# A causal mask moved from mask matmuls on TensorE to a GpSimd select after the exp, with new interleaving tables

## The chip, the cores and the metric

The kernel runs on one core of a Trainium2 chip. The metric is the device time of one execution in microseconds; "before" is the median of three runs.

## The reference, cut to what matters

The input is 16 sequences of 256 tokens with 128 channels, and it goes through nine residual layers: causal attention (16 heads of 8), a mixture of experts, causal attention, a grouped attention with a gated mixture of experts, linear attention, causal attention with an MLP, an arccos-kernel attention, and three blocks of quantised linear layers. Only the three causal attentions (stages `causal0`, `causal1`, `causal2`) are touched. Each computes, per head,

```python
a = einsum('bhqd,bhkd->bhqk', q, k) * hd ** (-0.5)
a = softmax(where(key > query, -1e9, a), axis=-1)
out = einsum('bhqk,bhkd->bhqd', a, v)
```

so what must be seen is that a probability is zero wherever its key is later than its query.

## The kernel before

**Passes and halves.** The sequences go in eight passes of two (512 tokens). Each pass has a FRONT list of stages (causal0, moe0, causal1, mqa, moe1) and a BACK list (linear, causal2, mlp, arccos, three blocks). The program has three parts: "fronts" (the fronts of two passes side by side), a loop of six turns called "both" (the front of one pass beside the back of another), and "backs" (two backs side by side). The two that run side by side are called halves; each has its own four PSUM banks and its own buffers.

**The order of work.** Each engine runs its instructions in program order. Every stage is a Python generator per engine that yields between steps, and `weave` takes steps from the two halves in turn by a table written out by hand for each engine and part (`PE_RUNS`, `ACT_RUNS`, `DVE_RUNS`): the numbers are how many steps come from one half, then from the other. A step contains its own semaphore waits, so a wait in one half's step holds up the other half's steps behind it on that engine.

**A causal stage.** It projects q, k and v, finds a row maximum for every query and head (`max_pe`, `max_dve`), and then works through 12 sets (`CSETS`) of three, three and two heads (`TRIOS`). A head has three score blocks of 128 keys by 128 queries: the earlier keys against both query tiles (256 columns), and the later keys against the later queries (128 columns), 384 columns in all (`HEADW`). Two of the three are diagonal blocks, in which half of the entries must be masked. For a set, `causal_scores_pe` waits until the exp of the set before has emptied the banks, writes the mask into the two diagonal blocks of each head by one bf16 matmul over 256 columns (line 837), and adds to it the scores (line 843) and the negated maximum (line 848). `causal_exp_act` (line 933) then takes the exp of all heads of the set in one ScalarE instruction, from PSUM into one of two `probs` buffers, and `causal_pv_pe` (lines 862 and 865) multiplies the probabilities by the values. On TensorE the step "probabilities by values" of set e-1 comes after the scores of set e, and the exp of set e+1 waits for it, since there are two buffers.

**GpSimd.** It only fills some constants at the start of the program.

## Time and profile before

| What | us |
|---|---|
| median of three runs | 3342.96 |
| lowest and highest | 3331.83, 3349.52 |
| profiled execution, span from first to last instruction | 3337.4 |
| TensorE matmul busy | 2641.8 |
| ScalarE busy | 1912.7 |
| VectorE busy | 1763.9 |
| GpSimd busy | 3.6 |
| mean granted TensorE clock, share of full speed | 0.795 |

The profiled execution's own time is given by its span alone, 5.6 us under the median of the runs. Matmuls are pipelined and their ends are modelled, so durations of neighbours overlap; the distance between two starts is the better measure of what one of them costs.

### The profile page before, as it was taken

What the parts mean: (1) busy time and instruction counts of PE and PEld (TensorE: products, weight loads), DVE (VectorE), ACT (ScalarE), POOL (GpSimd) and SP (SyncE); (2) the same over time, 40 slices, a digit from 0 to 9 for tenths busy, and PEclk for the clock granted to TensorE, in tenths of its full rate; (3) what the DMA queues carried; (4) which work ended last, traced back from release to release, by engine and by line L of the source; (5) the groups of instructions that cost most, each with busy time, mean ns of one, the idle gap of its engine ahead of it and who ended that gap; (6) DMA issues with size and microseconds to landing.
All of it is one profiled execution on the core that took longest, in us unless ns stands there. A gap on an engine that the chain in (4) does not pass through costs nothing.

```text
span 3337.4 us, 46425 instructions
## 1 busy us (share of the span) xinstructions
PE 2641.8 (79%) x18736; PEld 1529.0 (46%) x18736; DVE 1763.9 (53%) x2698; ACT 1912.7 (57%) x1960; POOL 3.6 (0%) x12
## 2 busy tenths in 40 slices
PE   8999999777997789877898688986889868897215
PEld 4666456343563435534355344553445534453102
DVE  5463574545656355553555545654455544563524
ACT  2433435875358753586445864468534685447994
POOL 0000000000000000000000000000000000000000
PEclk7997989659896588966899668986779867987557
DMA  3000000000000000000000000000000000000000
GB/s 128 2 1 1 20 1 1 1 1 8 1 1 1 1 8 1 1 1 0 8 1 1 1 0 8 2 1 1 0 5 2 1 1 0 4 1 1 0 0 6
DMA packets 4561, 18.68 MB, mean 6 GB/s; under 512 B 608, under 2 KB 864, under 8 KB 3808
## 3 DMA queue, kind: packets, MB, share of 16 engines
q1 hardware_dynamic: 4320, 15.38, 1.2%
q8 instruction: 162, 2.65, 0.3%
q14 instruction: 79, 0.65, 0.1%
HBM read 13.28 MB, written 2.10 MB: 5 GB/s over the span
## 4 chain that ended last, share of the span: by engine, by line
PE 54%; ACT 19%; DVE 15%; issue 12%; DVEq 0%; DMA 0%; ACTq 0%; SPq 0%
ACT back_cosines L1320 6%; PE one_ps L1164 2%; PE two_ps L1275 2%; PE one_ps L862 2%; PE two_ps L910 2%; ACT back_cosines L1322 2%; PE one_ps L1710 2%; DVE back_nsum L1330 2%; PE one_ps L1717 2%; ACT L1320 2%; PE one_ps L766 1%; PE one_ps L1723 1%; DVE back_cosines L1393 1%; ACT L1862 1%; PE two_ps L862 1%
## 5 line engine op out<-in xcount | busy, mean ns | idle before, releaser
L1320 ACT ACTIVATE back_cosines<-back_cosines 128x2048 f32<-128x2048 f32 x256 | 472.2, 1899 | 0.5
L933 ACT ACTIVATE front_scratch<-one_ps 128x1152 f32<-128x1152 f32 x168 | 171.5, 1021 | 225.0 <-PE one_ps L848 224.8
L1322 ACT ACTIVATE back_cosines<-back_cosines,wts 128x2048 f32<-128x2048 f32 x128 | 252.4, 1994 | 41.1 <-DVE back_cosines L1393 40.9
L1330 DVE TENSOR_REDUCE back_nsum<-back_cosines 128x8 f32<-128x2048 f32 x64 | 144.4, 2281 | 234.0 <-ACT back_cosines L1320 234.0
L797 DVE TENSOR_REDUCE front_negm<-one_ps 128x8 f32<-128x1024 f32 (+1 forms) x168 | 204.4, 1220 | 56.6 <-PE one_ps L772 55.5
L837 PE MATMUL one_ps<-ident_bf,mask_q 128*128 128x256 bf16 x480 | 93.3, 302 | 80.5 <-ACT front_scratch L933 69.3
L696 ACT ACTIVATE back_cosines<-two_ps,wts 128x512 fp32r<-128x512 f32 x28 | 19.3, 688 | 224.1 <-PE two_ps L910 224.1
L766 PE MATMUL one_ps<-front_qkr 32*128 32x128 f32 (+1 forms) x896 | 136.5, 414 | 14.1 <-issue 8.9
L1393 DVE TENSOR_SCALAR back_cosines<-two_ps 128x2048 f32<-128x2048 f32 x56 | 128.2, 2290 | 28.5 <-PE two_ps L1257 28.3
L933 ACT ACTIVATE back_cosines<-two_ps 128x1152 f32<-128x1152 f32 (+1 forms) x84 | 86.0, 1024 | 92.0 <-PE two_ps L848 92.0
L766 PEld LDWEIGHTS one_ps<-front_qkr 32*128 32x128 f32 x896 | 96.6, 274 | 88.5 <-DVE front_negm L797 46.3
L1275 PE MATMUL two_ps<-back_cosines,back_vs 128*18 128x256 f32 x896 | 79.5, 505 | 69.0 <-DVE back_vs L1342 69.0
L862 PE MATMUL one_ps<-front_scratch,one_v 128*18 128x256 f32 x896 | 116.7, 424 | 6.1 <-DVE front_split_parts L704 5.7
L772 PE MATMUL one_ps<-mask_q,ident_bf 128*128 128x512 bf16 (+1 forms) x360 | 119.4, 428 | 0.0
L843 PE MATMUL one_ps<-front_qkr 32*128 32x256 f32 (+1 forms) x896 | 105.8, 328 | 0.0
L797 DVE TENSOR_REDUCE back_cosines<-two_ps 128x4 f32<-128x1024 f32 (+1 forms) x84 | 97.9, 1216 | 8.8 <-PE two_ps L772 8.6
L837 PEld LDWEIGHTS one_ps<-ident_bf,mask_q 128*128 128x128 bf16 x480 | 39.2, 103 | 132.7 <-ACT front_scratch L933 92.1
L700 DVE TENSOR_SCALAR front_scratch<-one_ps,wts 128x512 fp32r<-128x512 f32 x77 | 57.4, 746 | 71.6 <-PE one_ps L865 56.0
L910 PE MATMUL two_ps<-back_cosines,two_v 128*18 128x128 f32 x896 | 77.8, 376 | 20.9 <-DVE back_split_parts L704 20.6
L1164 PEld LDWEIGHTS one_ps<-front_v,front_scratch 128*128 128x128 f32 x448 | 85.0, 291 | 13.0 <-issue 13.0
L953 DVE TENSOR_TENSOR back_cosines<-two_ps,wts 128x768 f32<-128x768 f32 (+1 forms) x84 | 72.6, 864 | 34.8 <-PE two_ps L883 34.8
L843 PEld LDWEIGHTS one_ps<-front_qkr 32*128 32x128 f32 x896 | 71.3, 208 | 42.1 <-issue 42.1
(630 smaller groups left out, 5795.1 us busy)
## 6 DMA issues: line engine op xcount, KB each, us to landing
wts<-w_dram SPq DMA_DIRECT2D x1, 4184.0 KB, 15.3
front_xin<-x_dram SPq DMA_DIRECT2D x8, 256.0 KB, 4.2
out_dram<-back_z SPq DMA_DIRECT2D x8, 256.0 KB, 2.1
wts<-w_dram SPq DMA_DIRECT2D x1, 1736.5 KB, 19.1
wts<-w_dram SPq DMA_DIRECT2D x1, 1199.0 KB, 5.3
wts<-w_dram SPq DMA_DIRECT2D x1, 1152.0 KB, 16.5
wts<-w_dram SPq DMA_DIRECT2D x3, 256.0 KB, 5.8
wts<-w_dram SPq DMA_DIRECT2D x1, 516.5 KB, 4.8
```

The lines of the kernel that those rows point to most:

```text
L766: nc.tensor.matmul(h.ps[:, j, gi * keys:(gi + 1) * keys], h.q4r[rows(j, QUAD), g0 + gi, b * SEQ + qt * P:b * SEQ + (qt + 1) * P], h.k4r[ro ...
L797: nc.vector.tensor_reduce(into, h.ps[:, js, :].rearrange("p j (g k) -> p j g k", k=keys), AX.X, ALU.max, negate=True).then_inc(h.max_done. ...
L843: nc.tensor.matmul(h.ps[:, k, into], h.k4r[rows(j, QUAD), g, keys], h.q4r[rows(j, QUAD), g, queries], start=False, stop=False, skip_group_ ...
L862: nc.tensor.matmul(h.ps[rows(j, V2), 3, b * SEQ:(b + 1) * SEQ], h.v18[:, 2 * b, GROUPS * j + g, :], h.probs[:, e % 2, k * HEADW:k * HEADW ...
L910: last = nc.tensor.matmul(h.ps[rows(j, V2), 3, b * SEQ + t * P:b * SEQ + (t + 1) * P], h.v18[:, 2 * b + t, GROUPS * j + g, :], h.probs[:, ...
L933: nc.scalar.activation(h.probs[:, e % 2, 0:n * HEADW].rearrange("p (k c) -> p k c", c=HEADW), h.ps[:, 0:n, 0:HEADW], ACT.Exp, scale=float( ...
L1164: last = nc.tensor.matmul(h.ps[:, 3, c:c + MV1], h.probs[:, (e - 1) % 2, w:w + P], h.v33[:, 2 * b + kt, :], start=(kt == 0), stop=(kt == 1 ...
L1275: last = nc.tensor.matmul(h.ps[rows(j, V2), 2 + g2, 0:SEQ], h.vs[:, kt, HPG * g2 + j, :], h.cosines[:, u % 2, w:w + SEQ], start=(kt == 0), ...
L1320: nc.scalar.activation(cosines, cosines, func, scale=scale).then_inc(h.arc_pass.sem, 1)
L1322: nc.scalar.activation(cosines, cosines, func, scale=scale, bias=C(bias)).then_inc(h.arc_pass.sem, 1)
L1330: nc.vector.tensor_reduce(h.nsum[:, kt, :].rearrange("p (g2 j) -> p j g2", g2=2), h.cosines[:, u % 2, kt * 4 * TOK:(kt + 1) * 4 * TOK].rea ...
L1393: nc.vector.tensor_scalar(h.cosines[:, u % 2, kt * 4 * TOK:(kt + 1) * 4 * TOK].rearrange("p (j t) -> p j t", j=HPG), h.ps[:], CLIP, CLIP_L ...
```

## The change

The mask matmuls of line 837 go. The score matmuls now start the accumulation themselves, and the first of them writes its 256 columns into blocks 0 and 2 of the bank, so that blocks 0 and 1 are the two diagonal ones. The exp writes the probabilities of a set with all diagonal blocks side by side at the front of the buffer (`p (t k q)`), unmasked. A new GpSimd step, `causal_keep_pool`, waits for the exp, sets the entries with a key later than the query to zero with one `affine_select` in place over the diagonal blocks (768 elements per partition for three heads, 512 for two), and raises a new semaphore `probs_kept`. The step that multiplies by the values waits for that semaphore in place of the exp's; the next set's scores still wait for the exp's. All tables of TensorE, ScalarE and VectorE are replaced, with the same number of steps in each, and GpSimd gets one. The part of the diff that isn't shown is the rest of these tables and the two unused generators for stages without work on GpSimd.

```diff
     "both": (
-        1, 2, 1, 1, 1, 1, 1, 1, 1, 1, 2, 1, 1, 2, 2, 2, 1, 2, 1, 1, 1, 3, 1, 2, 2, 1, 1, 3, 1, 2, 1, 5, 2, 1, 1,
-        2, 1, 2, 1, 1, 2, 1, 2, 1, 1, 2, 2, 2, 1, 2, 1, 1, 1, 2, 1, 2, 1, 1, 1, 2, 3, 2, 2, 1, 3, 2, 1, 2, 1, 2,
-        2, 2, 1, 2, 1, 2, 1, 4, 1, 3, 1, 4, 1, 1, 1, 1, 1, 3, 1, 1, 2, 1, 4, 3, 2, 4, 3, 1, 1, 1, 2, 4, 2, 1, 1,
-        1, 1, 4, 1, 4, 26, 1, 2, 2, 3, 2, 7, 1, 3, 2, 1, 2, 22, 2, 5, 1, 1, 1, 1, 5, 2, 2, 1, 1, 2, 1, 4, 1, 4,
-        2, 3, 1, 2, 1, 10, 1, 2, 2, 3, 1, 3, 1, 5, 1,
+        1, 2, 1, 1, 1, 1, 1, 1, 1, 1, 2, 1, 1, 3, 1, 2, 1, 5, 2, 1, 1, 2, 1, 2, 1, 2, 1, 2, 1, 2, 1, 2, 1, 1, 2,
+        2, 1, 2, 1, 1, 3, 1, 2, 1, 1, 1, 1, 1, 2, 3, 1, 3, 1, 1, 1, 1, 2, 2, 1, 1, 1, 1, 2, 2, 3, 1, 2, 6, 1, 2,
+        2, 2, 1, 1, 1, 4, 1, 4, 1, 4, 1, 1, 1, 4, 1, 1, 3, 1, 4, 2, 1, 1, 1, 3, 3, 2, 2, 1, 2, 4, 2, 2, 1, 1, 1,
+        5, 1, 2, 30, 1, 1, 2, 2, 2, 9, 1, 1, 2, 2, 1, 1, 1, 18, 2, 5, 1, 1, 1, 1, 3, 2, 1, 1, 4, 2, 1, 7, 1, 1,
+        2, 4, 1, 1, 1, 11, 1, 3, 2, 1, 2, 8, 1,
...
+POOL_RUNS = {
+    "fronts": (
+        7, 1, 1, 1, 1, 1, 1, 1, 2, 8, 5, 3, 2, 2, 3, 1, 1, 1, 1, 4, 2, 5, 2,
+    ),
+    "both": (
+        12, 12, 16,
+    ),
+    "backs": (
+        8, 2, 1, 1, 1, 4, 2, 5,
     ),
 }
...
+        self.probs_kept = signal("probs_kept", {s: CSETS for s in CAUSAL})
...
+        def score_tile(h, k, kt):
+
+
+            return h.ps[:, k, 0:HEADW].rearrange("p (n q) -> p n q", q=P)[:, 0:3:2, :] if kt == 0 else h.ps[:, k, P:2 * P]
+
+        def prob_tile(h, e, k, kt):
+
+
+            n = TRIOS[e % len(TRIOS)]
+            tiles = h.probs[:, e % 2, 0:n * HEADW].rearrange("p (t k q) -> p t k q", k=n, q=P)
+            return tiles[:, 0:3:2, k, :] if kt == 0 else tiles[:, 1, k, :]
+
         def causal_scores_pe(pe, h, turn, s):
             for e in range(CSETS + 1):
                 yield
...
-                    for k in range(len(heads)):
-                        diagonals = h.ps[:, k, :].rearrange("p (n q) -> p n q", q=P)[:, 0:4:2, :]
-                        nc.tensor.matmul(diagonals, mask_q[:], ident_bf[:].unsqueeze(1).broadcast_to([P, 2, P]),
-                                         start=True, stop=False, skip_group_check=True)
-                    for kt, into in ((0, slice(0, SEQ)), (1, slice(SEQ, HEADW))):
+                    for kt in range(2):
                         for k, (b, j) in enumerate(heads):
                             queries = slice(b * SEQ + kt * P, (b + 1) * SEQ)
                             keys = slice(b * SEQ + kt * P, b * SEQ + (kt + 1) * P)
-                            nc.tensor.matmul(h.ps[:, k, into], h.k4r[rows(j, QUAD), g, keys], h.q4r[rows(j, QUAD), g, queries],
-                                             start=False, stop=False, skip_group_check=True)
+                            nc.tensor.matmul(score_tile(h, k, kt), h.k4r[rows(j, QUAD), g, keys], h.q4r[rows(j, QUAD), g, queries],
+                                             start=True, stop=False, skip_group_check=True)
                         for k, (b, j) in enumerate(heads):
                             queries = slice(b * SEQ + kt * P, (b + 1) * SEQ)
                             minus_max = max_rows[rows(j, QUAD), g:g + 1].broadcast_to([QUAD, P])
-                            last = nc.tensor.matmul(h.ps[:, k, into], minus_max, h.maxTr[rows(j, QUAD), queries],
+                            last = nc.tensor.matmul(score_tile(h, k, kt), minus_max, h.maxTr[rows(j, QUAD), queries],
...
         def causal_pv_pe(pe, h, turn, s, e):
             g, heads = trio(e)
             yield
-            pe.wait_ge(h.probs_ready.sem, h.probs_ready.at(turn, s, e + 1))
+            pe.wait_ge(h.probs_kept.sem, h.probs_kept.at(turn, s, e + 1))
             if e % len(TRIOS) == 0:
                 if g > 0:
                     pe.wait_ge(h.part_ready.sem, h.part_ready.at(turn, s, g))
             for k, (b, j) in enumerate(heads):
                 nc.tensor.matmul(h.ps[rows(j, V2), 3, b * SEQ:(b + 1) * SEQ], h.v18[:, 2 * b, GROUPS * j + g, :],
-                                 h.probs[:, e % 2, k * HEADW:k * HEADW + SEQ], start=(b == 0), stop=False, skip_group_check=True)
+                                 prob_tile(h, e, k, 0), start=(b == 0), stop=False, skip_group_check=True)
             for k, (b, j) in enumerate(heads):
                 last = nc.tensor.matmul(h.ps[rows(j, V2), 3, b * SEQ + P:(b + 1) * SEQ], h.v18[:, 2 * b + 1, GROUPS * j + g, :],
-                                        h.probs[:, e % 2, k * HEADW + SEQ:(k + 1) * HEADW],
+                                        prob_tile(h, e, k, 1),
                                         start=False, stop=True, skip_group_check=True)
             last.then_inc(h.pv_ps.sem, 1)
 
@@ -930,8 +950,28 @@
                 act.wait_ge(h.score_ps.sem, h.score_ps.at(turn, s, e + 1))
                 if e >= 2:
                     act.wait_ge(h.pv_ps.sem, h.pv_ps.at(turn, s, e - 1))
-                nc.scalar.activation(h.probs[:, e % 2, 0:n * HEADW].rearrange("p (k c) -> p k c", c=HEADW),
-                                     h.ps[:, 0:n, 0:HEADW], ACT.Exp, scale=float(HD) ** -0.5).then_inc(h.probs_ready.sem, 1)
+                nc.scalar.activation(h.probs[:, e % 2, 0:n * HEADW].rearrange("p (t k q) -> p k t q", k=n, q=P),
+                                     h.ps[:, 0:n, 0:HEADW].rearrange("p k (t q) -> p k t q", q=P), ACT.Exp,
+                                     scale=float(HD) ** -0.5).then_inc(h.probs_ready.sem, 1)
+
+        def causal_keep_pool(pool, h, turn, s):
+
+
+            for e in range(CSETS):
+                n = TRIOS[e % len(TRIOS)]
+                yield
+                pool.wait_ge(h.probs_ready.sem, h.probs_ready.at(turn, s, e + 1))
+                pool.sem_inc(wait_carrier)
+                diagonals = h.probs[:, e % 2, 0:2 * n * P].rearrange("p (n q) -> p n q", q=P)
+                nc.gpsimd.affine_select(diagonals, diagonals, pattern=[[0, 2 * n], [1, P]], compare_op=ALU.is_ge, fill=0.0,
+                                        base=0, channel_multiplier=-1).then_inc(h.probs_kept.sem, 1)
+
+        def headed_pool(pool, h, turn, s):
+            if s in CAUSAL:
+                yield from causal_keep_pool(pool, h, turn, s)
+
+        def nothing_pool(pool, h, turn, s):
+            yield from ()
...
+            run(pool, POOL_RUNS, {"norm": nothing_pool, "causal": headed_pool, "linear": headed_pool, "mqa": nothing_pool,
+                                  "moe0": nothing_pool, "moe1": nothing_pool, "mlp": nothing_pool, "arccos": nothing_pool,
+                                  "block": nothing_pool})
```

## Rows read from the trace of the kernel before

**Rows 1.** The page: busy time of each engine, and the chain's shares

```profile
PE 2641.8 (79%) x18736; PEld 1529.0 (46%) x18736; DVE 1763.9 (53%) x2698; ACT 1912.7 (57%) x1960; POOL 3.6 (0%) x12
...
PE 54%; ACT 19%; DVE 15%; issue 12%; DVEq 0%; DMA 0%; ACTq 0%; SPq 0%
```

**Rows 2.** Windows, all instructions: start:end length, busy and count of each engine, clock

```profile
core 0: us, PE busy (x) PEld busy (x) DVE busy (x) ACT busy (x) POOL busy (x), PEclk, DMA share, GB/s
0.00:480.00 480.00, 436.98 (x3308) 272.34 (x3311) 263.04 (x466) 174.80 (x240) 3.56 (x12) 0.88 0.07 27
892.00:1304.00 412.00, 337.35 (x2362) 194.27 (x2358) 220.86 (x337) 241.05 (x247) 0.00 (x0) 0.79 0.01 2
2950.00:3337.00 387.00, 190.54 (x1300) 93.18 (x1300) 170.30 (x208) 292.27 (x235) 0.00 (x0) 0.69 0.01 2
```

**Rows 3.** Windows, line 837 (the mask matmuls) alone

```profile
0.00:480.00 480.00, 26.10 (x144) 12.24 (x144) 0.88 0.07 27
892.00:1304.00 412.00, 18.13 (x96) 7.57 (x96) 0.79 0.01 2
2950.00:3337.00 387.00, 11.66 (x64) 5.83 (x64) 0.69 0.01 2
sum 3337.00, PE 143.82 PEld 62.15; mean PE 17.98 PEld 7.77
```

**Rows 4.** Line 837: what TensorE sat idle for ahead of it

```profile
  ACT front_scratch L933: 165.8, 113
```

**Rows 5.** Timeline of two sets at the upper clock: start, length, instruction

```profile
501.05 0.50 PE L837 MATMUL two_ps<-ident_bf,mask_q 128*128 128x256 bf16 x3
501.48 0.39 PE L843 MATMUL two_ps<-back_qkr 32*128 32x256 f32 x3
...
502.09 0.62 PE L862 MATMUL two_ps<-back_cosines,two_v 128*18 128x256 f32 x6
502.20 1.13 ACT L933 ACTIVATE back_cosines<-two_ps 128x1152 f32<-128x1152 f32 x1 [0.90 <-PE two_ps L848]
...
503.51 0.39 PE L837 MATMUL two_ps<-ident_bf,mask_q 128*128 128x256 bf16 x2
```

**Rows 6.** The chain that ended last, 500 to 520: start, length, instruction

```profile
503.58 0.33 PE two_ps L837 x2
...
504.51 0.55 PE two_ps L862 x6
505.06 0.22 PE two_ps L865 x6
```

**Rows 7.** Timeline of a set at the lower clock

```profile
1041.53 0.82 PE L837 MATMUL one_ps<-ident_bf,mask_q 128*128 128x256 bf16 x3 [6.73 <-ACT front_scratch L933]
...
1042.28 0.58 PE L843 MATMUL one_ps<-front_qkr 32*128 32x256 f32 x3
...
1043.33 1.05 PE L862 MATMUL one_ps<-front_scratch,one_v 128*18 128x256 f32 x6
```

**Rows 8.** Windows of one turn of the loop, line 837 alone

```profile
1032.00:1052.00 20.00, 3.07 (x11) 0.98 (x11) 0.50 0.00 0
1052.00:1072.00 20.00, 3.61 (x19) 1.36 (x19) 0.88 0.01 2
1072.00:1092.00 20.00, 0.39 (x2) 0.11 (x2) 0.72 0.01 1
```

**Rows 9.** Windows of the same turn, all instructions, columns as in group 2

```profile
912.00:932.00 20.00, 18.98 (x197) 11.66 (x193) 9.00 (x30) 10.68 (x14) 0.00 (x0) 1.00 0.01 2
1032.00:1052.00 20.00, 10.82 (x85) 6.04 (x87) 4.47 (x4) 19.97 (x13) 0.00 (x0) 0.50 0.00 0
1052.00:1072.00 20.00, 16.49 (x213) 9.38 (x209) 15.65 (x16) 13.07 (x11) 0.00 (x0) 0.88 0.01 2
```

**Rows 10.** Timeline of GpSimd, all of whose work is at the start

```profile
0.74 1.06 POOL L1926 MEMSET one_v<- 128x1152 f32 x1 [0.29 <-POOLq L2093]
1.73 0.53 POOL L1927 MEMSET front_negm<- 128x512 f32 x1
```

**Rows 11.** Line 953, VectorE: duration ns min/median/max, first and last start, forms

```profile
L953 DVE TENSOR_TENSOR back_cosines<-two_ps,wts x84: 678/946/958, 420.2 to 2903.8; 128x768 f32<-128x768 f32 x56, 128x512 f32<-128x512 f32 x28
```

2 lines of the change are left out of this document (added), and 68 rows, old and new, of tables (ACT_RUNS, DVE_RUNS, PE_RUNS).

## The prediction

> **What bounds the kernel now.** I read the page first: TensorE is busy for four fifths of the span, ScalarE and VectorE for little more than half, GpSimd for nothing, and the chain that ended last lies on TensorE for 54%, on ScalarE for 19%, on VectorE for 15% [rows 1]. That is a mean over parts with different limits, so next came the windows. In "fronts" (0 to 480) TensorE is busy 437 of 480 us and bounds. A turn of the loop takes 412 us (892 to 1304 is the one I read), with TensorE at 337 and ScalarE at 241. "Backs" has TensorE at 191 of 387 and ScalarE at 292 [rows 2]. Inside the turn, at 912 to 932, TensorE is busy 18.98 of 20 us, while at 1032 to 1052, where causal1 runs beside the long exp passes of the arccos stage, it is ScalarE with 19.97 of 20 and TensorE has 10.82 [rows 9]. The reader is to see two kinds of place for a causal set: one where TensorE has no idle time, and one where its next set waits for a ScalarE that is busy with the other half.
>
> Then the line that goes: line 837 is busy 143.8 us in all, 26.1 in fronts, 18.1 in each full turn, 11.7 in backs [rows 3]. TensorE idled 165.8 us ahead of it for the exp of the front half's set before [rows 4]. So the mask matmuls stand in a loop of their own: exp, masks, scores, exp.
>
> **Removed: 768 mask matmuls.** The busy time overstates them, since matmuls overlap. From the first mask matmul to the first score matmul three of them take 501.48 - 501.05 = 0.43 us at full clock; their busy time is 0.50 [rows 5]. The chain gives two of them 0.33 us [rows 6]. At the lower clock three take 1042.28 - 1041.53 = 0.75 [rows 7]. Taking 0.07 off each of the 288 sets (3 stages x 8 passes x 12), 143.8 - 20.2 = 123.6 us of TensorE's time goes: 26.1 - 54 x 0.07 = 22.3 in fronts (144 mask matmuls are 54 sets), 11.66 - 24 x 0.07 = 10.0 in backs, and 91.3 in the loop. It is a maximum only if nothing else waits. Where does it count?
> - Fronts: TensorE bound for 91% of the time; 20 us.
> - Loop: of the 18.1 us in a turn, 3.07 lie at 1032 to 1052, where ScalarE is full: nothing comes of them. 4.00 more lie at 1052 to 1092 [rows 8], with ScalarE at 13.07 of 20 in the first half of it [rows 9]: I count half. That leaves (18.1 - 3.1 - 2.0) / 18.1 = 0.72 of 91.3, so 66 us.
> - Backs: the causal sets end there before the long ScalarE passes; 8 of 10 us.
> Together 94 us.
>
> **Added: 288 selects, and a wait.** The select has its engine to itself, so what counts is how late it makes the step on lines 862 and 865, and what stands behind that step in TensorE's queue: everything of both halves, the next scores included. The trace of before has no select. Below: GpSimd's memsets take 1.06 us for 1152 elements and 0.53 for 512 [rows 10], 0.83 ns an element, so 768 take 0.74. A select reads as well, so it is no faster. Above: three such passes (read, compare, write), 0.10 + 3 x 0.64 = 2.0; VectorE's 768-element pass with a second input takes 0.95 [rows 11], and twice that is 1.9. I take 1.1 us, between the same engine's row and twice it, nearer the first because the memset is a row of this engine; 0.74 and 2.0 stay for the range. To this I add 0.35 us for two semaphores, from the exp to GpSimd and from there to TensorE: an estimate, twice the 0.18 us from the end of an exp (502.20 + 1.13) to the matmul that waited for it (503.51) [rows 5].
>
> What does it do to a set? With full clock and three heads: scores until the next step 502.09 - 501.48 = 0.61, from the last of them to the exp 0.11, exp 1.13 [rows 5], values step 0.77 [rows 6]. Let w be the other half's work per set on TensorE. Before, a set takes the larger of 0.18 + 0.43 + 0.61 + 0.11 + 1.13 = 2.46 (the loop through the exp) and 1.81 + w (TensorE full). After, if nothing stands between the scores of e and the values step of e-1, that step can start 0.11 + 1.13 + 0.35 + S after the end of the scores of e-1, where S is the select, and the set takes the largest of 2.03, 1.38 + w, and half of (1.59 + S + 1.38 + w). For S = 1.1 and w = 0, 0.5 and 1 that is 2.04, 2.29 and 2.54 against 2.03, 2.03 and 2.38 without the wait: 0.14 us lost on average. For S = 0.74 it is 0.03, for S = 2.0 it is 0.59.
>
> How many sets have nothing between? That can be counted in the new table of TensorE, by writing out both halves' steps in its order: in the loop 21 of 33 such places in a turn (4 in causal0, 9 in causal1, 8 in causal2), 22 of 44 in fronts, 5 of 22 in backs, so 22 + 6 x 21 + 5 = 153. (By the old table 25, 37 and 18.) The others have at least one step of the other half between and I cost them at nothing; that step is the cover, and where it is taken away the set joins the 153 at 0.14 us. 153 x 0.14 = 22 us.
>
> The Trainium skill, "GPSIMD Engine Reference", section "Performance pitfalls for Q7 kernels", gives 1.03 to 2.03 cycles an element for a compare and select; at its 1.2 GHz an estimate of 0.66 to 1.30 us for 768 elements, by which the loss would be about 2 to 37 us. No run shown here has one.
>
> **Moved, at nothing.** The exp reads and writes the same elements in runs of 128, so its 1.13 us stays. Values steps read two runs of 128 columns where they read one of 256: same columns. VectorE and ScalarE keep their steps in number. The new tables as such are worth something I can't take from rows; I count zero and keep 25 us either way for them, about a fourth of what is at stake.
>
> Sum against the profiled execution: 3337.4 - 94 + 22 = 3265; the median is 5.6 us higher, which makes 3271. I say 3270.
>
> **Rivals.**
> 1. The select is slow, two passes or more. For it: the engine has done nothing but memsets here, and 1.9 us is twice VectorE's row. At S = 2.0 the loss is 153 x 0.59 = 90 us and the gain is gone: 3339. The Trainium skill, "GPSIMD Engine Reference", section "When to use GPSIMD", has VectorE about twice as fast for elementwise work with two inputs, and GpSimd near its line rate for one; by the first rule the select would be this rival, by the second it would not.
> 2. The other side, slower: from S = 2.0 on each further 0.1 us costs 153 x 0.05 = 8 us, and the covered sets begin to stall too. At S = 2.6 it is 153 x 0.89 = 136 us lost: 3343 - 94 + 136 = 3385. TensorE would show a wait for GpSimd ahead of most values steps.
> 3. The freed time isn't free: ScalarE's passes and VectorE's steps set the end in more of the loop than I counted, or the new tables don't use the gaps. For it: 165.8 us of idle time ahead of line 837, which is latency and not TensorE work. Against: that idle time is in the same loop that gets shorter by the masks. A third of the 94 us remains: 3312 without a stall, about 3323 with half of it.
> 4. The clock. The masks are dense work, and a TensorE that waits for GpSimd is idle in short pieces. At 912 to 932 it has 1.00 at 95% busy, at 1032 to 1052 it has 0.50 (1.2 GHz) at 54% [rows 9]. A set's scores take 1043.33 - 1042.28 = 1.05 us at the lower level [rows 7] against 0.61, and its values step about double 0.77: 1.2 us more for each set that changes level. 60 sets that do so cost the 72 us of the forecast: 3343.
>
> **How the numbers follow.** Forecast, S from 0.74 to 1.5 (where the formula gives 0.34 us a set, 52 us in all, and 3301): 0.72. Rival 1: 0.08. Rival 2: 0.06. Rival 3: 0.09. Rival 4: 0.05. A change of 0.5% is 17 us, about what a measurement of this kernel can tell from none. The forecast is all faster; of rival 3 0.04 is faster and 0.05 the same; rival 1 is the same; rival 2 and 0.04 of rival 4 are slower. That makes 0.76, 0.14 and 0.10. The range goes down to all 124 us and the tables' 25, 3343 - 149 = 3194, and I cut it at 3200; up it takes in rivals 1 and 3, to 3345. The likeliest case alone has 3225 to 3315.
>
> **What would show it.** The profile after should have no bf16 matmul in the score step, GpSimd busy 288 x about 1.0 = 290 us (between 200 and 520), a set of scores 0.43 us shorter, the turn of the loop at about 404 us in place of 412, fronts at about 463, and waits of line 862 for GpSimd of 30 us or so in total. If the select's mean is under 0.8 us the time should be below 3260; over 2 us, the prediction is wrong by step "added". If the select is short and the time isn't down, rival 3 holds, and if the mean clock falls below 0.77 in the loop, rival 4.

## The result, and the profile after

The changed kernel takes 3421.53 us (median; 3419.33 to 3425.81) against 3339.53 of the kernel before in the same session: a ratio of 1.0237, 95% interval [1.0207, 1.0266]. It is 2.4% slower. The prediction was 3270 us with a range up to 3345.

The page after, busy times and the chain that ended last, in the form of [rows 1]:

```profile
span 3419.3 us, 45758 instructions
PE 2627.1 (77%) x17968; PEld 1512.0 (44%) x17968; DVE 1768.7 (52%) x2698; ACT 1931.7 (56%) x1980; POOL 232.9 (7%) x300
...
PE 53%; DVE 19%; ACT 18%; issue 9%; POOL 0%; DVEq 0%; DMA 0%; ACTq 0%; POOLq 0%; SPq 0%
```

TensorE has its 768 instructions fewer, but only 14.7 us less busy time than in [rows 1], where the mask matmuls were busy for 143.8 [rows 3]. GpSimd has 0% of the chain (0.9 us in a turn of the loop); VectorE's share went from 15% to 19%. ScalarE has 20 instructions more, though no step was added on it.

The selects, grouped by shape (mean ns of one; idle time and releaser behind the bar), the longest of them in the timeline with the VectorE pass beside it, and what TensorE sat idle for ahead of the values step (the source view of its first line: us, times):

```profile
L966 POOL TENSOR_SCALAR_AFFINE_SELECT front_scratch<-front_scratch 128x768 f32<-128x768 f32 x128 | 110.8, 866 | 2297.9 <-ACT front_scratch L953 2297.8
L966 POOL TENSOR_SCALAR_AFFINE_SELECT front_scratch<-front_scratch 128x512 f32<-128x512 f32 x64 | 40.7, 637 | 141.2 <-ACT front_scratch L953 141.2
L966 POOL TENSOR_SCALAR_AFFINE_SELECT back_cosines<-back_cosines 128x512 f32<-128x512 f32 x32 | 22.6, 707 | 60.9 <-ACT back_cosines L953 60.9
...
971.82 2.29 DVE L1595 TENSOR_TENSOR front_qk<-front_split_parts,front_oh 128x2048 f32<-128x2048 f32 x1
972.21 2.40 POOL L966 TENSOR_SCALAR_AFFINE_SELECT back_cosines<-back_cosines 128x512 f32<-128x512 f32 x1 [3.55 <-ACT back_cosines L953]
...
  POOL front_scratch L966: 31.9, 42
...
  POOL back_cosines L966: 12.9, 34
```

So a select is 0.87 us for three heads and 0.64 for two (the mean of 0.71 in one group comes from a single one of 2.40 us beside a VectorE pass over two tensors), below the 1.1 that the prediction took. It holds TensorE up in 76 places for 44.8 us, of which next to nothing is in the chain. That speaks against the select as what made the kernel slower, and the experiments below settle it. Where the time went is read from SyncE's queue, which loads an input when the opening stretch ends and stores an output once a turn (start us, length):

```profile
430.01 0.34 SPq L1933 DMA_DIRECT2D front_xin<-x_dram  x1
840.33 0.36 SPq L1938 DMA_DIRECT2D out_dram<-back_z  x1
...
1260.17 0.35 SPq L1938 DMA_DIRECT2D out_dram<-back_z  x1
...
2509.45 907.81 SPq L1938 DMA_DIRECT2D out_dram<-back_z  x4
```

In the kernel before the same four stand at 403.12, 807.63, 1216.90 and 2442.80. The opening stretch ("fronts") is 27 us longer, and the four turns between the first store and the fifth take (2509.45 - 840.33) / 4 = 417.3 us each against 408.8. What follows the fifth store, 909.9 us against 894.6, still holds the last turn.

### The profile page after: what moved, and what is told of

Its sections match the earlier page's. It is cut to its first block, busy times and chain, and to the rows that moved or that the text cites. A ratio compares the mean times of both kernels' runs of the same rounds, so it can differ in the third digit from the quotient of the medians.

```text
span 3419.3 us, 45758 instructions
## 1 busy us (share of the span) xinstructions
PE 2627.1 (77%) x17968; PEld 1512.0 (44%) x17968; DVE 1768.7 (52%) x2698; ACT 1931.7 (56%) x1980; POOL 232.9 (7%) x300
## 4 chain that ended last, share of the span: by engine, by line
PE 53%; DVE 19%; ACT 18%; issue 9%; POOL 0%; DVEq 0%; DMA 0%; ACTq 0%; POOLq 0%; SPq 0%
ACT back_cosines L1360 5%; ACT back_cosines L1362 3%; PE one_ps L778 3%; PE one_ps L882 3%; PE two_ps L1315 2%; PE one_ps L784 2%; PE one_ps L1204 2%; DVE back_cosines L1433 2%; DVE back_nsum L1370 2%; DVE front_negm L809 2%; PE two_ps L569 2%; PE two_ps L930 2%; PE one_ps L863 2%; PE one_ps L1750 2%; ACT L1360 1%
## 5 line engine op out<-in xcount | busy, mean ns | idle before, releaser
L966 POOL TENSOR_SCALAR_AFFINE_SELECT front_scratch<-front_scratch 128x768 f32<-128x768 f32 (+1 forms) x192 | 151.4, 790 | 2439.1 <-ACT front_scratch L953 2439.0
L863 PE MATMUL one_ps<-front_qkr 32*128 32x256 f32 (+1 forms) x896 | 118.0, 355 | 49.5 <-ACT front_scratch L953 35.5
L1315 PE MATMUL two_ps<-back_cosines,back_vs 128*18 128x256 f32 x896 | 96.6, 604 | 76.5 <-DVE back_vs L1382 76.5
L882 PE MATMUL one_ps<-front_scratch,one_v 128*18 128x256 f32 x896 | 137.0, 491 | 17.0 <-POOL front_scratch L966 8.5
L778 PEld LDWEIGHTS one_ps<-front_qkr 32*128 32x128 f32 x896 | 99.2, 280 | 88.6 <-DVE front_negm L809 45.2
L863 PEld LDWEIGHTS one_ps<-front_qkr 32*128 32x128 f32 x896 | 80.6, 232 | 109.8 <-ACT front_scratch L953 62.9
L966 POOL TENSOR_SCALAR_AFFINE_SELECT back_cosines<-back_cosines 128x768 f32<-128x768 f32 (+1 forms) x96 | 78.0, 813 | 416.2 <-ACT back_cosines L953 416.2
L1204 PEld LDWEIGHTS one_ps<-front_v,front_scratch 128*128 128x128 f32 x448 | 94.4, 321 | 18.4 <-issue 18.4
L1204 PE MATMUL one_ps<-front_v,front_scratch 128*128 128x33 f32 x448 | 97.8, 394 | 4.3 <-DVE front_scratch L1126 4.3
L868 PE MATMUL one_ps<-front_maxTr,max_rows 32*128 32x256 f32 (+1 forms) x896 | 96.8, 329 | 0.0
```

The source lines that it names most:

```text
L778: nc.tensor.matmul(h.ps[:, j, gi * keys:(gi + 1) * keys], h.q4r[rows(j, QUAD), g0 + gi, b * SEQ + qt * P:b * SEQ + (qt + 1) * P], h.k4r[ro ...
L863: nc.tensor.matmul(score_tile(h, k, kt), h.k4r[rows(j, QUAD), g, keys], h.q4r[rows(j, QUAD), g, queries], start=True, stop=False, skip_gro ...
L882: nc.tensor.matmul(h.ps[rows(j, V2), 3, b * SEQ:(b + 1) * SEQ], h.v18[:, 2 * b, GROUPS * j + g, :], prob_tile(h, e, k, 0), start=(b == 0), ...
L966: nc.gpsimd.affine_select(diagonals, diagonals, pattern=[[0, 2 * n], [1, P]], compare_op=ALU.is_ge, fill=0.0, base=0, channel_multiplier=- ...
L1204: last = nc.tensor.matmul(h.ps[:, 3, c:c + MV1], h.probs[:, (e - 1) % 2, w:w + P], h.v33[:, 2 * b + kt, :], start=(kt == 0), stop=(kt == 1 ...
```

## The experiments

All times below are ratios to the kernel before on the same chip and in the same session, since its median moved between 3337.6 and 3345.2; 0.001 is 3.3 us. "Front end" is the input load that ends "fronts", "turn" the mean of four turns, both from the one profiled execution of each run. That execution can lie off the median: for e1 it was the fastest of ten, 19 us under it. And the front end of e6, whose tables for fronts are the old ones, is 13 us later than that of e1. So small differences in these two columns carry little.

| run | median us | ratio, 95% interval | front end | turn |
|---|---|---|---|---|
| changed kernel | 3421.5 | 1.0237 [1.0207, 1.0266] | 430.0 | 417.3 |
| e1 select, old tables | 3344.3 | 1.0014 [0.9992, 1.0036] | 400.9 | 408.8 |
| e2 masks, new tables | 3465.6 | 1.0385 [1.0348, 1.0421] | 439.7 | 422.1 |
| e3 neither, old tables | 3302.4 | 0.9900 [0.9866, 0.9934] | 398.6 | 403.6 |
| e4 neither, new tables | 3423.7 | 1.0246 [1.0221, 1.0271] | 439.0 | 417.2 |
| e5 e1 with filler matmuls | 3345.6 | 1.0028 [1.0006, 1.0051] | 396.0 | 409.7 |
| e6 new tables in the loop alone | 3401.6 | 1.0182 [1.0147, 1.0218] | 413.5 | 418.1 |
| e7 new tables in fronts alone | 3367.5 | 1.0060 [1.0037, 1.0083] | 430.4 | 407.8 |
| e8 changed kernel, half the row maximum | 3411.0 | 1.0232 [1.0176, 1.0289] | 435.1 | 413.0 |
| e9 e1, half the row maximum | 3293.4 | 0.9896 [0.9841, 0.9951] | 388.9 | 401.9 |
| e10 loop new, then old | 3358.5 | 1.0046 [1.0025, 1.0067] | 400.1 | 413.0 |
| e11 loop old, then new | 3373.2 | 1.0084 [1.0055, 1.0113] | 395.3 | 413.9 |
| e12 e1, three places | 3633.5 | 1.0879 [1.0855, 1.0904] | 445.1 | 448.9 |
| e13 masks, three places | 3683.7 | 1.1029 [1.0996, 1.1063] | 447.2 | 453.1 |
| e14 e1, ScalarE's later order new | 3474.6 | 1.0415 [1.0385, 1.0445] | 400.9 | 431.5 |
| e15 neither, three places | 3630.6 | 1.0867 [1.0838, 1.0897] | 436.7 | 449.7 |
| e16 e1, values one step later | 3518.7 | 1.0533 [1.0500, 1.0565] | 419.8 | 433.5 |
| e17 three places, values behind scores | 3582.8 | 1.0734 [1.0703, 1.0764] | 446.0 | 441.2 |
| e18 changed kernel, one stretch put back | 3413.6 | 1.0239 [1.0201, 1.0277] | 437.4 | 413.9 |

**Mask, select and tables taken apart (e1 to e4).** e1 is the changed kernel with the TensorE, ScalarE and VectorE tables of before; e2 the kernel before with the new ones; e3 and e4 have neither mask nor select and wait for the exp directly:

```diff
-            pe.wait_ge(h.probs_kept.sem, h.probs_kept.at(turn, s, e + 1))
+            pe.wait_ge(h.probs_ready.sem, h.probs_ready.at(turn, s, e + 1))
```

> The code of the changed kernel with the order tables of before for TensorE, ScalarE and VectorE; GpSimd's table gives the selects in the order in which the old table of ScalarE has the exps. Theory T (the new tables lost the time, the select itself saves some): 3250 to 3310 us, faster than before by 1 to 3%. Theory W (the values step's wait for the select is the cause, whatever the order): 3400 us or more, since the old tables have 136 + 6 x 1 more places with nothing between the scores and the values step. Theory M (the masks were never on the path and the tables are neutral): 3340.

> The code of before, with its mask matmuls and no select, in the new order of TensorE, ScalarE and VectorE. Theory T: the masks come on top of a worse order, 3440 to 3520 us. Theory W: no wait for a select, so about 3340. Theory M: as the changed kernel or less, 3340 to 3420.

> Old tables, no mask matmuls and no select at all: the probabilities stay unmasked, and the values step waits for the exp. This is the most that taking the masks away can give in the old order. By my sum it should be 94 us under before, 3245. Theory T: 3230 to 3280. Theory W: the same, with the select variant far above it. Theory M: 3340.

> New tables, no mask matmuls and no select: the probabilities stay unmasked, and the values step waits for the exp. The difference from the changed kernel is the price of the wait for the select in the new order. Theory T: small, 3380 to 3410. Theory W: the whole loss and the masks' time come back, 3250 to 3300.

Measured: the new tables cost 0.0385 with masks, 0.0346 with neither and 0.0223 with the select: 129, 116 and 74 us. That is the loss, and it needs no select. In the old order, removing the masks brings 33 us (e3) and the select takes 38 of them back (e1 against e3). In the new order the masks' removal brings 46 us and the select costs nothing (e4 against the changed kernel, intervals overlap). Theory T holds for where the loss is, but not for its gain: e1 was to be 1 to 3% faster than before and is level with it, and e3 was to be at 3230 to 3280 and is at 3302. Theory M's 3340 is met by e1 alone; e2 and e3 rule it out.

The two orders can be compared with the same instructions in both. In the profiled executions of before and e2 TensorE is busy for 2641.8 and 2697.2 us and idle for 695.6 and 765.5: of 125 us more, 55 are longer matmuls and 70 are idle time. For e3 and e4 it is 81 and 48 of 129.

Why 33 us, where the masks were busy for 143.8? Line groups of TensorE, before, in e3 and after (busy us, mean ns of one), with the source view of the values line before and after (ns min/median/max):

```profile
L862 PE MATMUL one_ps<-front_scratch,one_v x896: 376/391/634, 59.9 to 2722.3; 128*18 128x256 f32 x180
...
L862 PE MATMUL one_ps<-front_scratch,one_v 128*18 128x256 f32 x896 | 116.7, 424 | 6.1 <-DVE front_split_parts L704 5.7
L843 PE MATMUL one_ps<-front_qkr 32*128 32x256 f32 (+1 forms) x896 | 105.8, 328 | 0.0
```

```profile
L882 PE MATMUL one_ps<-front_scratch,one_v 128*18 128x256 f32 x896 | 126.0, 455 | 15.6 <-DVE front_split_parts L716 15.6
L863 PE MATMUL one_ps<-front_qkr 32*128 32x256 f32 (+1 forms) x896 | 113.5, 339 | 87.1 <-ACT front_scratch L953 76.5 <-DVE front_maxTr L716 9.8
```

```profile
L882 PE MATMUL one_ps<-front_scratch,one_v x896: 376/392/634, 62.5 to 2778.4; 128*18 128x256 f32 x180
...
L882 PE MATMUL one_ps<-front_scratch,one_v 128*18 128x256 f32 x896 | 137.0, 491 | 17.0 <-POOL front_scratch L966 8.5 <-DVE front_split_parts L716 8.0
L863 PE MATMUL one_ps<-front_qkr 32*128 32x256 f32 (+1 forms) x896 | 118.0, 355 | 49.5 <-ACT front_scratch L953 35.5 <-DVE front_maxTr L716 13.3
```

The mean of the same matmuls got longer: a values matmul took 424 ns, 455 without masks, 491 after. Minimum, median and maximum stayed at 376, 391 and 634, so it isn't that each got longer: more of them run at the lower of the two clock levels (0.50, as in [rows 9]). Of the 1536 values matmuls over 256 columns, 154 take over 600 ns before, 308 in e3, 291 in e2, 428 in e4, 365 in e1 and 456 after, and nearly all others about 385. Before, all 154 began while the granted clock was 0.50 and none of the others did; after, it was so for 443 of the 456 and for 13 of the others (counted in the traces). TensorE's busy time fell by 2641.8 - 2557.9 = 83.9 us in e3 and not by 143.8. Some 20 of the missing 60 are the overlap that the prediction took off itself; the line groups of all other matmuls add up to 36 us more than before. And of the 83.9 not all is time won: TensorE's idle time rose from 695.6 to 740.7 us. Three windows over the same stretch of "fronts", of before, e3 and after (columns of [rows 2], last but two the granted clock), show what goes with it:

```profile
12.00:403.00 391.00, 366.19 (x2750) 232.69 (x2749) 211.35 (x389) 144.16 (x200) 0.00 (x0) 0.89 0.05 18
```

```profile
12.00:403.00 391.00, 363.91 (x2627) 231.58 (x2625) 210.97 (x389) 147.04 (x205) 0.00 (x0) 0.86 0.06 21
```

```profile
12.00:403.00 391.00, 353.56 (x2562) 228.35 (x2561) 196.81 (x368) 137.34 (x192) 37.70 (x48) 0.82 0.04 17
```

TensorE is as busy in e3 as before with 123 matmuls fewer, at 0.86 of full speed and not 0.89. "Fronts", for which the prediction counted 20 us, got 403.1 - 398.6 = 4.5 shorter.

**Does the clock hold the rest (e5)?** Three bf16 matmuls over 256 columns, adding zero to the values bank, ahead of TensorE's wait for the exp in 7 of 12 sets of e1, 504 in all:

```diff
                     else:
+                        if e % 3 != 1:
+                            for k in range(3):
+                                nc.tensor.matmul(h.ps[:, 3, 0:SEQ], zero_bf[:].broadcast_to([P, P]), ident_bf[:].unsqueeze(1).broadcast_to([P, 2, P]),
+                                                 start=False, stop=False, skip_group_check=True)
                         pe.wait_ge(h.probs_ready.sem, h.probs_ready.at(turn, s, e))
```

> The select with the old tables (3344 us), and ahead of the scores' wait for the exp, in 7 of 12 sets, three bf16 matmuls of 256 columns of zeros added into the values bank, which change nothing in it. They cost 0.43 us of TensorE at the upper clock, 168 sets, 72 us in all, but stand where TensorE often idles for the exp (211 us in all). Theory C (without the masks TensorE spends more of the causal stages at the lower clock, and that gives back most of what their removal saves): mean clock up from 0.782 to about 0.80 and the time within 15 us of 3344. Rival (the clock plays no part, the masks only filled idle time): clock as before, time up by 20 to 50 us.

The mean clock went from 0.782 to 0.798 (the medians over the runs of each are 0.777 and 0.793). A values matmul is back at the 424 ns of before, and 156 of 1536 take over 600 ns:

```profile
L886 PE MATMUL one_ps<-front_scratch,one_v 128*18 128x256 f32 x896 | 116.1, 424 | 22.8 <-DVE front_split_parts L716 16.1 <-POOL front_scratch L970 6.7
```

TensorE was busy for 2595.3 us against e1's 2591.3, although the filler alone is 89.4 of it: the other matmuls took 85 us less. Its idle time is 735 us against 732, so the filler didn't fill idle time; the clock that it bought paid for it, and no more. The time is e1's (1.0028 and 1.0014, intervals overlap). So dense work in these places raises the clock, and the masks did the same; but to raise it with filler brings nothing. Whether filler would help in the new order was not run.

**Which part of the tables (e6, e7).**

> The changed kernel with the new tables in the loop alone, the old ones in fronts and backs. By the turns in the traces (417.3 against 408.8 us) the new loop order costs 6 x 8.5 = 51 of the 77 us: 3395. If the loss is in fronts and backs: 3350 to 3365.

> The select code with the new tables in the opening stretch of two fronts alone, old ones in the loop and the backs. The x load that ends that stretch came at 430.0 us with all new tables and at 400.9 with the old ones, so this run should be slower by that: 3365 to 3375 us. If the order of the opening stretch costs nothing by itself and the 29 us come from what it hands to the loop, 3340 to 3350.

Against e1 the loop's tables cost 0.0168 (56 us), those of fronts 0.0046 (15 us; in the profiled executions the front end is 29 us later). Together that is 0.0214 of the 0.0223, so the backs' tables cost nothing that shows.

**Are VectorE's row maxima now in the way (e8, e9)?** In the new order the matmuls of the maxima (lines 778 and 784 on TensorE) lie on the chain for about 31 us a turn against 12, VectorE's reduces behind them for about 10 in both. Both runs leave out half of the columns of each reduce and leave the matmuls as they are:

```diff
-                nc.vector.tensor_reduce(into, h.ps[:, js, :].rearrange("p j (g k) -> p j g k", k=keys),
+                nc.vector.tensor_reduce(into, h.ps[:, js, :].rearrange("p j (g k) -> p j g k", k=keys)[:, :, :, 0:keys // 2],
```

> The changed kernel, but the row maximum is taken over half of the columns only, so a reduce of 1.22 us takes about 0.68 (the softmax's shift is another one and the output with it). VectorE loses about 150 us of work. Theory D (the new order puts the reduces of VectorE on the path): 60 to 100 us faster than the changed kernel, 3320 to 3360. Rival (the new order loses by TensorE's own idle and clock): about 20 to 40 us faster, as in the old order.

> The same half reduce in the select kernel with the old tables (3344 us). Theory D: 20 to 40 us faster, 3305 to 3325, half or less of what it brings in the new order. Rival: the same gain in both orders.

A theory that fell: it gains nothing that can be told in the new order (1.0232 against 1.0237) and 39 us in the old one (0.9896 against 1.0014). So it isn't VectorE's reduces that the new order suffers from. The matmuls, which are what grew on the chain, were not changed in any run.

**Which part of a turn (e10, e11).** One table for each engine that changes from one order to the other where the front half is in moe0 and the back half at the start of mlp.

> The select code with the old tables outside the loop and, in each turn of it, the new order of TensorE, ScalarE and VectorE up to the point where the front half is in moe0 and the back half at the start of mlp (that is, through causal0 and causal2), and the old order from there on (arccos, causal1, mqa, moe1 and the blocks); GpSimd's table is the new one of the loop. Theory L, that the new order is good where it goes around the select and loses its time in the stages behind: the new order was 1 to 4 us ahead of the old one at that point of a turn (129 against 132 us for the last exps of causal2), so a turn comes to 405 to 408 us against 408.8 with the old order all through, and the kernel to 3320 to 3345 us. Rival G, that the loss comes from the front and back halves' causal stages as laid out anew (its later part only shows what was displaced): the turn stays near 417 us and the time at 3390 to 3400. Rival E, that any order fitted to one part is only good with its other part: over 3360 us in this run and in the converse one.

> The converse: select code, old tables outside the loop, in each turn the old order through causal0 and causal2 and the new one behind it (arccos, causal1, mqa, moe1, blocks), GpSimd's old table. Theory L: all of the loop's loss is here, so about 3395 to 3410 us, turn near 417 to 420, and the count of function-table loads on ScalarE rises by most of the 20 that the new tables add. Rival G: near 3345 us with a turn of 409. Rival E: over 3400 here and over 3360 in the converse run.

The second part loses 0.0070 (23 us). The first loses 0.0032 (11 us), with intervals that just overlap; the new order isn't the better one there, and the second part alone is at 3373 us and not at the 3395 to 3410 of theory L. So L is wrong in its first half and has the second too large. The rest of the loop's loss, 0.0168 - 0.0102 = 0.0066 (22 us), appears only when both parts are new.

**Is it ScalarE's order there (e14, e18)?** The new order makes ScalarE change its function table more often, without any step being added: line groups of e1 and of the changed kernel,

```profile
L1360 ACT ACT_TABLE_LOAD x48 | 61.6, 1283 | 0.9
L1775 ACT ACT_TABLE_LOAD x27 | 34.6, 1283 | 1.3 <-PE one_ps L1750 0.9
```

```profile
L1360 ACT ACT_TABLE_LOAD x56 | 71.8, 1283 | 1.0
L1775 ACT ACT_TABLE_LOAD x33 | 42.3, 1283 | 7.6 <-PE one_ps L1750 7.2
```

188 loads in all against 168, 1.283 us each: 25.7 us. One place is where the front half's mqa begins. ScalarE's timeline there, in the changed kernel and then in e1 (line 1360 is an arccos pass of the back half, 1213 and 1217 mqa's copies of q and v):

```profile
1133.94 0.61 ACT L607 ACTIVATE front_sq<-front_sq 128x512 f32<-128x512 f32 x1
1134.58 1.28 ACT L1360 ACT_TABLE_LOAD   x1
1135.87 5.51 ACT L1360 ACTIVATE back_cosines<-back_cosines 128x2048 f32<-128x2048 f32 x3
1141.39 1.28 ACT L1360 ACT_TABLE_LOAD   x1
1142.69 1.91 ACT L1360 ACTIVATE back_cosines<-back_cosines 128x2048 f32<-128x2048 f32 x1
1144.51 0.58 ACT L1213 ACTIVATE front_qk<-one_ps 128x512 f32<-128x512 f32 x1
1144.98 0.27 ACT L1217 ACTIVATE front_v<-one_ps 128x128 f32<-128x128 f32 x1
```

```profile
1093.63 0.61 ACT L607 ACTIVATE front_sq<-front_sq 128x512 f32<-128x512 f32 x1
1094.27 1.28 ACT L1360 ACT_TABLE_LOAD   x1
1095.56 1.91 ACT L1360 ACTIVATE back_cosines<-back_cosines 128x2048 f32<-128x2048 f32 x1
1097.38 0.58 ACT L1213 ACTIVATE front_qk<-one_ps 128x512 f32<-128x512 f32 x1
1097.85 1.90 ACT L1360 ACTIVATE back_cosines<-back_cosines 128x2048 f32<-128x2048 f32 x1
1099.65 0.27 ACT L1217 ACTIVATE front_v<-one_ps 128x128 f32<-128x128 f32 x1
```

From the norm's last step to the copy of v it is 11.0 us in the new order and 6.0 in the old. VectorE's first maxima of mqa, in the same turn of each, come 306.2 and 298.7 us after the store that begins the turn (302.8 and 298.6 in the next one), behind 7.13 and 1.58 us of idle time:

```profile
1146.57 1.29 DVE L1240 TENSOR_REDUCE front_negm<-one_ps 128x2 f32<-128x512 f32 x2 [7.13 <-PE one_ps L1164]
```

```profile
1100.72 1.29 DVE L1240 TENSOR_REDUCE front_negm<-one_ps 128x2 f32<-128x512 f32 x2 [1.58 <-PE one_ps L1164]
```

> The select code with old tables, except that in each turn ScalarE's order alone is the new one behind causal0 and causal2; TensorE and VectorE keep the old order. With the new order of all three there the kernel took 3373 us, 29 more than with the old, and had 12 more loads of a function table on ScalarE (15.4 us). If the loads, or ScalarE's order as such, are the cause: 12 more loads here too, and 3360 to 3375 us. If TensorE's or VectorE's order is: 3340 to 3350, with or without the loads.

> The changed kernel with one stretch of ScalarE's order in the loop as it was before: where the front's mqa begins. In the changed kernel ScalarE runs four of the back's arccos passes (1.9 us each) and an extra load of its function table (1.28 us) between the norm ahead of mqa and mqa's copies of q and v, so that VectorE's maxima for mqa begin 303.1 us into a turn against 298.2 in the old order; until there the new order is not behind. The four passes go back to one ahead of the copy of q and one between q and v. Theory S (this place makes the loss of the loop's later part, 29 us over six turns in the run old then new): the turn comes from 417.3 down to about 412.5, function-table loads fall by 6 to 12, and the time by 25 to 35 us, to 3387 to 3400. Rival P (TensorE's and VectorE's new orders lose as much, and ScalarE's place is only where it shows): within 10 us of the changed kernel, 3410 to 3425.

e14 has 12 more loads and is 0.0401 (134 us) slower than e1: ScalarE's new order behind TensorE's and VectorE's old one is far worse than all three new (e11, 23 us). Its outcome is outside both expectations, and it tells no more than that the three tables are one thing. e18, with the stretch put back as it was, has 6 loads fewer and a turn of 413.9 instead of 417.3, 3.4 us; but its front end was 437.4 against 430.0 in a part that it doesn't touch, and the ratio, 1.0239, is the changed kernel's, as rival P has it. The place costs some 3 us a turn by the trace, a third of the 8.5, and the times don't show it. Theory S, with 25 us or more, fell.

**Can the select be hidden (e12, e13, e15 to e17)?** Sets of three, three and two heads fill 8 x 384 = 3072 columns, just the `probs` buffer, so that three places fit. In e12, e13 and e15 the values of set e-2 follow the scores of e, with the scores one step of the table earlier:

```diff
-            for e in range(CSETS + 1):
-                yield
+            for e in range(CSETS + 2):
+                if e <= CSETS:
+                    yield
...
-                if e > 0:
-                    yield from causal_pv_pe(pe, h, turn, s, e - 1)
+                if e > 1:
+                    yield from causal_pv_pe(pe, h, turn, s, e - 2)
```

> The select code with the old tables, and three places for the probabilities in turn instead of two (they fit in the same buffer, since sets of 3, 3 and 2 heads come in turn), with the values step of a set issued one set later: scores of e+2, then values of e. The select of a set then runs beside the next set's exp instead of ahead of a step that TensorE is at. Theory W (the select's 42 us in the old order, 3344 against 3302 with neither mask nor select, are its latency in the chain exp, select, values): most of it goes, 3300 to 3315 us, faster than the kernel before; waits of the values step for GpSimd fall to near nothing, select still about 0.87 us each. Rival C (the select's price is the clock, which is lower where TensorE has less to do, or GpSimd taking SBUF time from VectorE): still 3340 to 3350. Rival D (the later values step holds up the part that VectorE takes from its bank, and the group's end comes later): over 3350.

> The kernel before (mask matmuls, no select) with the same three places and the values step one set later: the control. Nothing stands between exp and values there, so theory W expects little, 3325 to 3345 us; if the later values step helps by itself (TensorE no longer waits for an exp ahead of values), it is up to 20 us faster, and then the gain of the run with the select is to be read less this.

> Neither mask nor select (the output is not causal within diagonal blocks), old tables, with the three places and the later values step: the floor for the run with the select. Theory W: equal to the two-place run without mask (3302 us) within 10, and the select run lies within 10 us above it.

With a set's time between exp and values the select costs 0.0012, 4 us with overlapping intervals (e12 against e15), where in e1 it cost 38. Theory W expected that, and says that the 38 us are latency ahead of the values step. That isn't shown. The select costs nothing in the changed kernel either, where nothing was put between. And e1 and e3, which differ by the select alone, have TensorE idle for 731.9 and 740.7 us and busy for 2591.3 and 2557.9 with the same 17968 matmuls: e1 waits for GpSimd ahead of the values in 56 places, 23.4 us in all, half of the changed kernel's 44.8, and what is longer is its matmuls, at a clock of 0.782 and not 0.787 (medians over the runs 0.777 and 0.786). So what the select costs in the old order reaches the time mostly as longer matmuls at a lower clock; why it does so there and not in the new order is open. One difference can be seen: in e1 six selects of the back half take 1.6 to 2.3 us, each beside a pass of VectorE over 2048 elements of two tensors (lines 1590 and 1595, 2.29 us), in the changed kernel one. That is some 7 us of GpSimd, too little for 38 by itself.

The shift itself costs 290 us (e12 against e1), and with the masks in place of the select 344 (e13 against before, for which theory W expected 3325 to 3345). Each scores step now stands where its exp may not be done, and 290 us is about one exp (1.02 us) for each of 288 sets; that this is the reason is argued and not shown.

e16 and e17 leave the scores where they were and move only the values, in e16 to the head of the next scores step (two places), in e17 behind its scores (three places):

```diff
+                if e > 1:
+                    causal_pv_pe(pe, h, turn, s, e - 2)
                 if e < CSETS:
...
-                    yield from causal_pv_pe(pe, h, turn, s, e - 1)
+                    yield
+                if e == CSETS:
+                    causal_pv_pe(pe, h, turn, s, e - 1)
```

> The select code with the old tables and two places for the probabilities. Every scores step stays where it is in TensorE's order; the values of a set are issued one step of the table later, at the head of the step that holds the next scores, so that what TensorE waits for there (the exp of the set after) is later than the select of this one. In the run with three places the scores had moved ahead by one step, to where their exp was not ready, and the loop's turn went from 409 to 449 us; with that shift the select cost nothing (3633 against 3631 without it). Theory W: with scores where they were, the select's 42 us go and little comes in its place: 3300 to 3325 us, faster than the kernel before. Rival D: the values now stand between TensorE and the scores in every set, 0.6 us of matmuls that ran beside an exp before, and VectorE gets each part of the output later: 3345 to 3400.

> As the run of values in the next step, but with three places for the probabilities and the values issued behind the scores of the same step, so that they run beside the exp that these scores release. Theory W: 3295 to 3320 us, at or a few us under the run with values ahead of scores. Rival D, parts reach VectorE later: 3345 to 3400 in both runs. If only the order within the step matters, this run is faster than the other by up to 0.3 us for each of 288 sets where TensorE comes late, some 50 us.

They are 173 and 240 us slower than e1, beyond rival D's own range. The values steps alone, each one step of its half later on one engine, cost more than masks and select together. What a misplaced values step does is seen in VectorE's waits for it (e1, then e16, then the changed kernel; us in total, times, longest):

```profile
DVE front_scratch L712 <- PE one_ps L885: 46.7, 24, 4.7
```

```profile
DVE front_scratch L712 <- PE one_ps L888: 124.0, 30, 9.2
```

```profile
DVE front_scratch L712 <- PE one_ps L885: 149.4, 32, 14.3
DVE back_cosines L712 <- PE two_ps L885: 70.4, 20, 6.0
```

Summed over all such rows of both halves, VectorE waits for the values step 96 us before, 82 in e1, 105 in e10, 180 in e11, 205 in e6, 237 in the changed kernel, 222 in e16 and 319 in e12. It isn't a price by itself (e14 has 87), and part of it stands where the engine had nothing to do anyway. VectorE's timeline in causal1 of the changed kernel and of e1:

```profile
1087.91 0.75 DVE L712 TENSOR_SCALAR front_scratch<-one_ps,wts 128x512 fp32r<-128x512 f32 x1 [14.25 <-PE one_ps L885]
1088.70 0.75 DVE L716 SCALAR_TENSOR_TENSOR front_split_parts<-one_ps,wts,front_scratch 128x512 fp32r<-128x512 f32 x1
1089.36 2.28 DVE L1370 TENSOR_REDUCE back_nsum<-back_cosines 128x8 f32<-128x2048 f32 x1
```

```profile
1041.15 2.29 DVE L1370 TENSOR_REDUCE back_nsum<-back_cosines 128x8 f32<-128x2048 f32 x1 [15.20 <-ACT back_cosines L1360]
```

The longest wait of the changed kernel, 14.25 us, holds the arccos reduction back until 1089.36, 2 us after ScalarE's pass for it ended (1087.09); in e1 VectorE waits 15.20 us at the same place for ScalarE. So this wait holds up some 2 us of VectorE's work and not 14. How the order's loss adds up from such places was not found.

## Why the prediction was wrong

**The sum.** The prediction had -94 for the masks, +22 for the select and 0 for the tables. Measured, step by step from before over e3 and e1 to the changed kernel: -33, +38 and +74, together 79 us slower.

**Step "Moved, at nothing": failed, and it decides.** It counted the new tables at zero, "and keep 25 us either way for them". They cost 129 us by themselves (e2), 116 without a mask (e4) and 74 with the select. The view that would have warned is in [rows 1]: no engine above 79%, so that the time of a kernel of two interleaved halves can come from the order and not from one engine's work. The term had no row behind it, and its bound was chosen from the size of the other terms and not from what an order can do; e16 shows 173 us from one step by one place.

**Step "Removed", 94 us: the mechanism right, the size wrong.** Measured 33 us in the old order, 46 in the new. The step took the 123.6 us that the masks occupy as time won wherever TensorE is busy. In e3 the other matmuls took 36 us more in total. There 308 and not 154 of the 1536 values matmuls ran at the lower clock; 154 are about 29 sets, and at the prediction's own 1.2 us for each set that changes level that is an estimate of 35 us. And of the 83.9 us that TensorE's busy time fell by, 45 went into idle time. The first is rival 4's mechanism, to which the prediction gave 0.05; the second is rival 3's, "the freed time isn't free", which put a third of the 94 us as what remains. A third is what e3 has.

**Step "Added", 22 us with S = 1.1: the select's length was too high, its price too low.** S is 0.87. A set of the changed kernel at the upper clock (start us, length):

```profile
496.39 1.12 ACT L953 ACTIVATE front_scratch<-one_ps 128x1152 f32<-128x1152 f32 x1
...
497.68 0.87 POOL L966 TENSOR_SCALAR_AFFINE_SELECT front_scratch<-front_scratch 128x768 f32<-128x768 f32 x1 [3.94 <-ACT front_scratch L953]
```

From the exp's end (497.51) to the select it is 0.17 us, and from a select's end to the values step that waited for it 0.06 (e1, 497.79 to 497.85), so the two semaphores are 0.23 and not 0.35. With these two the prediction's formula gives a loss of 0.08 us at w = 0.5 (half of 1.47 + 0.87 + 1.38 + 0.5, less 2.03) and none at w = 0 and 1: 4 us for 153 places. In the old order the select costs 38 us, 0.13 for each of 288 sets, and in the new one nothing that shows. The count of open places, 25 of 33 in a turn by the old table and 21 by the new, doesn't explain that; it stays open. What the formula has no term for is the clock, and by e1 against e3 that is where the select's cost comes out. From the Trainium skill, "GPSIMD Engine Reference", section "Performance pitfalls for Q7 kernels", the prediction estimated 0.66 to 1.30 us for this select; the trace agrees, with 0.87.

**Rivals.** Rivals 1 and 2 needed a select of 2 us and more and are out. Rival 3 named the mechanism in half a sentence, "the new tables don't use the gaps", but priced it as a part of the gain not had, never as a loss. Its test in the profile, "the select is short and the time isn't down", is what came. Rival 4 came too, beside it: from 154 to 456 of the 1536 values matmuls at the lower clock is 57 more sets, where it asked for 60, and the mean clock fell from 0.795 to 0.776 (in the loop from 0.795 to 0.774, just above its sign of 0.77). But it isn't the waits for GpSimd that did most of it: of the 302 more, 154 come with the masks' removal (e3), 120 with the tables (e4) and 28 with the select. The 120 are 22 sets, some 27 us at 1.2 us each, of the 116 that the tables cost without a mask; the rest is other matmuls and idle time, and what of it the clock holds is not separated. e5 shows only that to raise the clock again with filler brings no time in the old order.

**Small ones.** GpSimd's busy time, 290 us foreseen, is 232.9; the turn, 404 foreseen, 417.3; "fronts", 463 foreseen, ends at 430, but the prediction's window of 480 us was too long, since the part ends at 403 in the kernel before; the score step has no bf16 matmul, as said. TensorE's waits for GpSimd, about 30 foreseen, are 44.8.

**What stays open.** 56 of the 74 us lie in the loop, about 11 of them in the first part of a turn, 23 in the second and 22 in their meeting; inside these parts one place was tried, and it accounts for some 3 us a turn in the trace and nothing sure in the time. That fronts got later was measured (27 us in the trace, 15 in the time of e7) and not explained. No version with the select beats the kernel before as long as the row maximum is whole: e1, the select in the old order, is level with it. e9, with half of the maximum's columns, is 1% faster than before (0.9896), but its shift is no longer the true maximum.

## What to carry to other kernels

Where no engine is above 80% and two streams of work are woven by a table, the table is the most valuable thing in the kernel: price a new one by running it with the old code, before anything else, and give it a bound of some per cent and not zero. Work taken from TensorE is worth its time only where the same matmuls keep their length: compare the mean duration of untouched lines, the count of those at the lower clock, and the clock of a window, before counting it. What an added wait costs depends on the order that it stands in (38 us and nothing, for the same select), and need not be its own idle time; but to move a step out of its way can cost several times that.

## What was not expected of the hardware

- 504 dense bf16 matmuls added ahead of TensorE's waits left its busy time at 2595 us for 2591, its idle time at 735 for 732 and the kernel's time where it was, with the mean clock at 0.798 for 0.782: the other matmuls got 85 us shorter.
- A matmul's mean duration moved from 424 to 491 ns with its minimum, median and maximum within 1 ns of what they were (376, 391, 634), by how many of them ran at the lower clock.
- A select takes 866 ns for 768 elements and 637 for 512. In six traces (after, e1, e5, e11, e12, e16) every select of more than 1.1 us, up to 2.40, stands beside a 2.3 us pass of VectorE over two tensors of 2048 elements, which itself keeps its length; not every select beside such a pass is longer.
- A changed order of ScalarE's steps alone brought 20 more loads of its function table, 25.7 us of the engine, that no step of the code shows.
